# Working on the first 512 rows of expert 0 in plain fp32 between the last routing steps of a fused adaLN, scan and MoE kernel

## The reference

```python
h = _layernorm(x) * (1 + ca) + sa
x = x + ga * attn(h)          # gates, a scan over the sequence, a projection
h = _layernorm(x) * (1 + cb) + sb
x = x + gb * ffn(h)
# ffn:
gate_scores = softmax(h @ Wg + bg)
topk_scores, topk_idx = top_k(gate_scores, 2)         # renormalised
for e in range(8):
    y = gelu(h @ W1[e] + b1[e]) @ W2[e] + b2[e]       # 256 -> 1024 -> 256
    output = output + y * combine_w[..., e:e + 1]
```

## Time and profile before

| | |
|---|---|
| median of 3 runs | 806.8 us (803.32 to 809.53) |
| the profiled execution | 802.3 us, its span 800.5 us |
| PE matmul busy | 713.6 us, 89% of the span |
| DVE, ACT, POOL busy | 568.1, 408.6, 406.2 us |
| chain that ended last | PE 57%, DVE 22%, issue 10%, DMA 5%, POOL 3% |

### The profile page before, as it was taken

How to read it: one execution, slowest core, us unless ns; L and a number is a source line. 1 busy time by engine, 2 the same in 40 slices (tenths; PEclk the granted TensorE clock), 3 DMA queues, 4 the chain that set the end, 5 groups by cost and what they waited for, 6 DMA issues and landing times.

```text
span 800.5 us, 17260 instructions
## 1 busy us (share of the span) xinstructions
PE 713.6 (89%) x4850; PEld 657.7 (82%) x4850; DVE 568.1 (71%) x1793; ACT 408.6 (51%) x1024; POOL 406.2 (51%) x312
## 2 busy tenths in 40 slices
PE   4899999889799993489999899998898998989992
PEld 1777888778688873389999899998898998989992
DVE  6879899899988777665555755566875566585551
ACT  5364545435353332255655555664564664565660
POOL 1364637674744735654544544554653553554543
PEclk9899999999999997589999999999998999999997
DMA  8531104020101117334356334574542553534432
GB/s 291 179 114 54 54 5 143 14 94 28 54 22 61 47 35 237 118 100 69 69 116 131 54 62 78 114 179 106 158 64 54 118 128 56 115 57 75 66 68 41
DMA packets 50165, 72.56 MB, mean 91 GB/s; under 512 B 5792, under 2 KB 41964, under 8 KB 49968
## 3 DMA queue, kind: packets, MB, share of 16 engines
q0 software_dynamic: 16480, 27.28, 19.0%
q1 hardware_dynamic: 33616, 44.46, 17.8%
HBM read 48.85 MB, written 22.87 MB: 90 GB/s over the span
## 4 chain that ended last, share of the span: by engine, by line
PE 57%; DVE 22%; issue 10%; DMA 5%; POOL 3%; ACT 2%; SPq 0%; DVEq 0%; POOLq 0%; ACTq 0%
PE yb L913 19%; PE mm L903 19%; PE mm L759 11%; PE yb L784 3%; DMA gbr<-mod_rows,xm 3%; DVE ob L1008 2%; PE tp L886 1%; DVE rsn L941 1%; DVE bst L945 1%; DVE rt L1042 1%; DVE mm L1005 1%; DVE mm L1002 1%; DVE SL L235 1%; DVE nt L940 1%; POOL gbr L536 1%
## 5 line engine op out<-in xcount | busy, mean ns | idle before, releaser
L736 ACT ACTIVATE h<-mm,b1T 128x256 f32<-128x256 f32 (+1 forms) x288 | 134.2, 466 | 166.7 <-PE mm L903 123.4
L541 POOL DMA_INDIRECT out_x<-ysb,tokb x68 | 115.1, 1692 | 203.2 <-DVE ysb L1271 166.9
L1240 DVE TENSOR_TENSOR hl<-h,hh 128x256 fp32r<-128x256 f32 (+1 forms) x288 | 122.0, 427 | 105.0 <-ACT hh L737 102.3
L903 PE MATMUL mm<-fh,SH 128*128 128x256 f32 x576 | 165.6, 287 | 9.3 <-DVE fl L1206 9.1
L913 PE MATMUL yb<-SH,hh 128*128 128x256 f32 x544 | 158.7, 292 | 12.8 <-DVE hl L1240 12.6
L903 PE MATMUL mm<-fl,SH 128*128 128x256 f32 x576 | 163.9, 285 | 0.0
L903 PE MATMUL mm<-fh,SL 128*128 128x256 f32 x576 | 163.7, 284 | 0.0
L913 PE MATMUL yb<-SL,hh 128*128 128x256 f32 x544 | 155.1, 285 | 0.0
L913 PE MATMUL yb<-SH,hl 128*128 128x256 f32 x544 | 155.0, 285 | 0.0
L737 ACT ACTIVATE hh<-mm,b1T 128x256 fp32r<-128x256 f32 (+1 forms) x288 | 133.5, 464 | 0.0
L903 PEld LDWEIGHTS mm<-fh,SH 128*128 128x128 f32 x576 | 112.2, 195 | 11.1 <-issue 11.1
(11 more groups left out here) (206 smaller groups left out, 1203.5 us busy)
## 6 DMA issues: line engine op xcount, KB each, us to landing
xin<-disp_x SPq DMA_DIRECT2D x74, 132.0 KB
wraw<-in_L_ffn_W SPq DMA_DIRECT2D x8, 1024.0 KB, 5.3
h2all<-in_L_ffn_W SPq DMA_DIRECT2D x8, 1024.0 KB, 5.6
xb<-in_L_attn_x SPq DMA_DIRECT2D x8, 512.0 KB, 3.7
out_x<-x2b SPq DMA_DIRECT2D x8, 512.0 KB, 3.0
mb<-mod_rows SPq DMA_DIRECT2D x3, 768.0 KB, 6.2
wraw<-in_L_attn_W_ugg SPq DMA_DIRECT2D x1, 1536.0 KB, 10.2
gbr<-mod_rows,xm POOLq DMA_INDIRECT x74, 3.8
```

The costliest lines, as they stand in the source:

```text
L541: e.indirect_dma_start(out=out_rows, out_offset=bass.IndirectOffsetOnAxis(ap=tokb[:, j:j + 1], axis=0), in_=ysb[:, j, :], in_offset=None, ...
L736: e.activation(h32[:, f % 2, c_], mm[f % 4][:, c_], ACT.Gelu_apprx_tanh, bias=bias)
L903: i = e.matmul(mm[f % 4][:, 0:TE], a[:, k, f * 128:(f + 1) * 128], b[:, k, :], start=(k == 0 and t == 0), stop=(k == 1 and t == 2))
L1240: e.tensor_tensor(hl[:, f, w_], h32[:, f % 2, w_], hh[:, f, w_].bitcast(F32), ALU.subtract)\
```

## The change

Once the groups 0 to 4 have been sent, the first 512 rows of expert 0's region in `Xd` are loaded to `xinE`, and all of their work is done in plain fp32 from the raw weights (`w1raw`, `w2raw`), on PE between the routing steps of the groups 6 and 7. In stage two expert 0 starts at row `skip` = min(512, rows that it has by group 4).

- SP: `xinE` is loaded in four DMAs ahead of the last `store_x2`. The first tile of expert 0 now waits for all sends.
- PE in group 7: a count (`early_count`), and eight transposes (`turn_early`) between the two parts of `main_part(7, 3, ...)`. After `logits(6)`: seven blocks of layer 1 (`early_layer1`, 2 matmuls of 128x512), `turn_h2(7)`, the eighth block, `rank(6)`, `logits(7)`, two blocks of layer 2 (`early_layer2`, 4 matmuls of 128x256), `rank(7)`, one block, the total count, five blocks.
- ACT: two copies (`early_rows`); eight GELUs of 128x512 (`early_gelu`), each followed by one `split_high` of expert 0; `h2t_copy(7)` stands ahead of the last, and both `gate_sigmoid` behind it. 
- DVE: three small operations in `place(5)`, `early_weights` (six) ahead of `add_y(7)`, `early_out` (two of 128x512, four of 128x256) after `counts`.
- POOL: four gathers (`gbrE`) behind `send(5, 1)`, ahead of its three `split_low`; and four accumulating indirect DMAs with the early rows' results, each of which waits until the one before has landed, between `pads_done` and tile 0 of the loop.

The diff, cut to what the prediction speaks of (tile declarations, PSUM addresses and iota columns are left out):

```diff
@@ sp_program
+            e.wait_ge(S["early_known"], 1)
+            e.reg_load(r_early, skipi[0:1, 1:2])
+            e.wait_ge(S["sent0"], 16 * 8 * 4)
+            e.wait_ge(S["sent1"], 16 * 8 * (EARLY_GROUPS - 4))
...
+            for j in range(4):
+                e.reg_mov(r_block, 128 * j)
+                e.reg_alu(r_block, r_block, r_early, ALU.min)
+                e.dma_start(xinE[:, j, :], Xd[bass.ds(e.snap(r_block, min_val=0, max_val=CAP - 128), 128), :])\
+                    .then_inc(S["early_loaded"], 16)
             store_x2(NG - 1)
...
-            with e.If_ne(r_late, 0):
-                e.wait_ge(S["sent2"], 16 * 8 * 2)
-                e.wait_ge(S["counts_ready"], 1)
-                e.reg_load(r_last, nmint[0:1, 0:1])
+            e.wait_ge(S["sent1"], 16 * 8 * (EARLY_GROUPS - 4))
+            e.wait_ge(S["sent2"], 16 * 8 * (NG - EARLY_GROUPS))
+            e.wait_ge(S["counts_ready"], 1)
@@ pool_program
             send(g - 2, 1)
+            e.wait_ge(S["early_meta"], 1)
+            for j in range(4):
+                e.indirect_dma_start(out=gbrE[:, j, :], out_offset=None, in_=modd.rearrange("b (n d) -> (b n) d", d=D),
+                                     in_offset=bass.IndirectOffsetOnAxis(ap=xmE[:, j, 5:6].bitcast(I32), axis=0))\
+                    .then_inc(S["early_gb"], 16)
             for q in range(5, 8):
                 split_low(e, 0, q)
@@
             e.sem_inc(S["pads_done"], 1)
+            for j in range(4):
+                e.wait_ge(S["early_ready"], j + 1)
+                past(e, "early_sent", 16 * j)
+                e.indirect_dma_start(out=out_rows, out_offset=bass.IndirectOffsetOnAxis(ap=tokE[:, j:j + 1], axis=0),
+                                     in_=ysbE[:, j, :], in_offset=None, compute_op=ALU.add).then_inc(S["early_sent"], 16)
+            e.wait_ge(S["early_sent"], 64)
             for n in range(E):
@@ act_program
+            def early_gelu(f):
+                e.wait_ge(S["early_hidden"], f + 1)
+                if f >= 5:
+                    e.wait_ge(S["x2_ready"], NG)
+                e.activation(hE[:, f, :], mm[f % 2][:, :], ACT.Gelu_apprx_tanh, bias=vT[:, f:f + 1])\
+                    .then_inc(S["early_gelu"], 1)
@@
             h2t_copy(g - 1)
-            for q in range(8):
-                split_high(e, 0, q)
+            for f in range(NF):
+                if f == NF - 1:
+                    h2t_copy(g)
+                early_gelu(f)
+                split_high(e, 0, f)
             gate_sigmoid(g - 1)
-            h2t_copy(g)
             gate_sigmoid(g)
@@ pe_program
+            def turn_early():
+                e.wait_ge(S["early_loaded"], 64)
...
+            def early_layer1(f):
...
+                past(e, "early_gelu", f - 1)
+                for k in range(2):
+                    i = e.matmul(mm[f % 2][:, :], w1raw[:, k, f * 128:(f + 1) * 128], fE[:, k, :],
+                                 start=(k == 0), stop=(k == 1))
+                i.then_inc(S["early_hidden"], 1)
+
+            def early_layer2(f):
+                e.wait_ge(S["x2_ready"], NG)
+                e.wait_ge(S["early_gelu"], f + 1)
+                for j in range(4):
+                    i = e.matmul(yb[j // 2][:, (j % 2) * D:(j % 2 + 1) * D], hE[:, f, j * 128:(j + 1) * 128],
+                                 w2raw[:, f, :], start=(f == 0 and j % 2 == 0), stop=(f == NF - 1),
+                                 skip_group_check=True)
+                i.then_inc(S["early_summed"], 1)
@@
                 if not last:
                     turn_xn(g + 1)
+                else:
+                    turn_early()
                 main_part(g, 3, 1)
@@
             logits(g - 1)
+            for f in range(NF - 1):
+                early_layer1(f)
             turn_h2(g)
+            early_layer1(NF - 1)
             rank(g - 1)
             logits(g)
+            early_layer2(0)
+            early_layer2(1)
             rank(g)
+            early_layer2(2)
...
+            for f in range(3, NF):
+                early_layer2(f)
@@ dve_program, place
-                if g == NG - 2:
-                    e.tensor_scalar(lateint[0:1, 0:1], rt[0:1, 2, 0, 0:1], float(TE), None, ALU.is_lt)\
-                        .then_inc(S["late_ready"], 1)
+                if g == EARLY_GROUPS:
+                    e.wait_ge(S["early_counted"], 1)
+                    yield from lk(e, e.tensor_scalar(skip[:, :], tp[1][:, 0:1], float(EARLY), None, ALU.min), "dve_b")
+                    yield from lk(e, e.tensor_copy(skipi[:, 0:1], skip[:, :]), "dve_b")
+                    e.tensor_scalar(skipi[:, 1:2], tp[1][:, 0:1], -128.0, 0.0, ALU.add, ALU.max)\
+                        .then_inc(S["early_known"], 1)
@@
+            early_weights()
             add_y(g)
@@
             counts()
+            early_out()
```

More of the change, by code:

```diff
@@ L20 @@
 TE = 256
+EARLY = 512
+EARLY_GROUPS = 5
 MW = 8
@@ L140, in build @@
                 SL[i] = sb(p2, f"SL{i}", [128, 4096], F32R)
+            xinE = sb(p2, "xinE", [128, 4, DW])
+            gbrE = sb(p2, "gbrE", [128, 4, D])
+            fE = sb(p2, "fE", [128, 2, EARLY])
+            hE = sb(p2, "hE", [128, NF, EARLY])
             xin = sb(p2, "xin", [128, 2, DW])
@@ L387, in tile @@
                     load(rows_of)
-                    if first and n == 0:
-                        e.wait_ge(S["counts_ready"], 2)
-                        e.reg_load(r_last, nmint[0:1, n:n + 1])
                     if first and n + 2 < E:
                         split_done(e, n)
+                        if n == 0:
+                            e.wait_ge(S["early_summed"], NF)
                         load_w1(n + 2)
@@ L860, in pe_program @@
                     rank(g - 2)
+                if last:
+                    early_count()
                 main(g, 2)
@@ L1131, in counts, with early_weights, early_out @@
                 e.tensor_copy(kpk[:, :], kf[:, 0:2]).then_inc(S["counts_ready"], 1)
-                link(e, e.tensor_reduce(kf[:, 2:3], nf[:, 1, :], AX, ALU.min), "dve_a")
-                e.tensor_scalar(few[:, :], kf[:, 2:3], 0.0, None, ALU.is_lt).then_inc(S["few_ready"], 1)
+            def early_weights():
+                a, b, c_ = (wslE[:, q, :, :] for q in range(3))
+                e.wait_ge(S["early_loaded"], 64)
+                e.tensor_copy(xmE[:, :, :], xinE[:, :, D:DW]).then_inc(S["early_meta"], 1)
+                e.wait_ge(S["early_meta"], 1)
+                at = xmE[:, :, 2:4]
+                link(e, e.tensor_copy(tokE[:, :], xmE[:, :, 4].bitcast(I32)), "dve_a")
+                link(e, e.tensor_tensor(a, at, nomE.unsqueeze(2).to_broadcast([128, 4, 2]), ALU.is_ge), "dve_a")
+                link(e, e.scalar_tensor_tensor(b, at, float(CAP), a, ALU.is_lt, ALU.mult), "dve_a")
+                link(e, e.tensor_tensor(c_, b, xmE[:, :, 0:2], ALU.mult), "dve_a")
+                link(e, e.tensor_reduce(wE[:, :], c_, AX, ALU.add), "dve_a")
+            def early_out():
+                e.wait_ge(S["early_summed"], NF)
+                e.wait_ge(S["b2_loaded"], 16)
+                for q in range(2):
+                    e.tensor_tensor(ysbE[:, 2 * q:2 * q + 2, :], yb[q][:, :].rearrange("p (j d) -> p j d", j=2),
+                                    bc(b2b[:, 0, :], 2), ALU.add).then_inc(S["early_taken"], 1)
+                e.wait_ge(S["early_taken"], 2)
+                e.wait_ge(S["early_gb"], 64)
+                for j in range(4):
+                    e.scalar_tensor_tensor(ysbE[:, j, :], ysbE[:, j, :], wE[:, j:j + 1], gbrE[:, j, :],
+                                           ALU.mult, ALU.mult).then_inc(S["early_ready"], 1)
             weave(ln1_stats(0))
@@ L1234, in tile @@
                     if first:
-                        mark(e.tensor_scalar(nom[:, :], nom0, float(n * CAP), None, ALU.add))
+                        mark(e.tensor_scalar(nom[:, :], nom0, float(n * CAP) if n else skip[:, :], None, ALU.add))
                         due("dve_c", 1)
```

82 lines of the change are left out of this document (61 added, 21 removed).

## The result

The changed kernel takes 819.6 us (median of 4 runs, 817.95 to 820.34) where the kernel before takes 806.9 (4 runs, 803.32 to 809.53): the ratio is 1.015, 95% interval 1.011 to 1.019. The forecast was 816.5. Two executions on the third chip of the experiments, 2456.6 us of the kernel before and 905.5 us of the kernel without adds, lie far outside all others and are left out of every ratio.

A forecast was written before the change was run, and what follows sets the result against it. PE, busy 713.6 of 800.5 us with one hole at 300 to 350, where a chain of waits sets the end. -8.5 (start and tiles) + 18.2 (stall and clock) = +9.7: profiled 802.3 becomes 812, median 806.8 becomes 816.5; range 804 to 823.

The forecast's parts named there:

- three signs of being wrong or of another rival: First matmul of tile 0 after 360; group 6's first send after 329.6; clock of 0.50 within layer 1's seven blocks.
- the late sends: Rival: group 6's sends come later than booked and shift everything; +16 us, 823 us; chance 0.09.
- The stall: POOL's four chained adds delay tile 1's gathers: DVE waits 18.4 us, PE 15.9; 18.2 in the sum with the clock.
- The rival without a stall: DVE's wait is met earlier or PE's work in hand covers it; -8.5 us, 798.3 us; chance 0.12.
- that of the short stall: Adds land faster or overlap in issue, 2.7 us each; stall shrinks by 6.4, +3.3, 810 us; chance 0.14.
- Entry: PE in group 7: waiting for and turning the early rows ends the projections 1.1 us later (bounds +0.3 and +3).
- DVE's 4.29 us: A tiny DVE operation before `h2_ready_last` took 4.29 us during POOL's three `split_low`; moving these wins 4.1 us on DVE.
- ACT, the weights of group 6: `gate_sigmoid(6)` stands behind GELU 7 and a table load, so group 6's first send is at 327.6, +3.0 (bounds +1, +5).
- the table load: On ACT, the sigmoid's table must come back after the GELU; one load is 1.28 us.
- Start and tiles: Stage two: tile 0 starts at 356.8, tiles cost 11.72 us, two full tiles go; half tile starts 8.5 us earlier.
- The sum: Whole kernel: -8.5 (start and tiles) + 18.2 (stall and clock) = +9.7 us; 816.5 us on the median.

The follow-up runs named there:

- number 5: Changed kernel with both cures of the stall: the four adds right behind the last group's gather and without waits between them; 794.7 us, ratio 0.992, second chip.
- number 8: Changed kernel with two fp32 blocks ahead of group 7's turns, routing before most others, adds behind the gather and unchained; 789.2 us (second chip), 799.5 (third).
- experiment 4: Changed kernel with expert 1's two 1 MB weight loads held back until PE has signalled the eighth early hidden block; 819.9 us, ratio 1.016.

## Why the prediction came out, point by point

- **The whole, right in its range and its mechanism, with some luck in the number.** The prediction gave three signs of being wrong or of another rival, and they came: the first matmul of tile 0 after 360 (365.42), the first send of group 6 after 329.6 (336.72), and a clock of 0.50 within layer 1's seven blocks (0.50 from 318 to 322). So the late sends, which had a chance of 0.09 and 823 us, came in beside the stall. From profile to profile the miss is 8.1 us (812 forecast, 820.1 measured). The medians hide part of it, since the kernel before has a median 4.5 us above its profiled execution: 816.5 forecast, 819.6 measured.
- **The stall, right.** Forecast: DVE waits 18.4 us, PE 15.9, with the clock 18.2 in the sum. Measured: 17.8 and 16.3 in the trace, and 16.8, 19.2 and 16.9 us by leaving out or curing the adds. PE stood from 395.3 to 411.6 (forecast 386 to 402), later by the late sends. The four adds took 18.4 us until the splits start (forecast 17.2). The rival without a stall and that of the short stall are out. The estimate by the figure of the Trainium skill (DMA: Bandwidth & Descriptors, Anatomy of one DMA, SWDGE path), 2.3 us an add, is too short here too: the adds landed 3.7 to 4.7 us after issue.
- **Entry, too dear.** I booked +1.1 us. SP's four loads went out at 291.46 and the turns at 295.9 had no wait; PE's idle time before the turning of group 6 shrank from 1.22 to 0.27, and the projections began at 300.95 instead of 301.20: nothing.
- **DVE's 4.29 us, right**: with `split_low` away it was gone, and its modulation of the last group began at 313.32 instead of 317.34.
- **ACT, the weights of group 6: the order right, the size wrong in the profile after.** +3.0 us was forecast; it was +12.1 (336.72 against 324.62). The step had the order, the table load (1.28 at 332.40) and the pace right: where signals are prompt, the send is 2.2 us later than before, counted from the projections. What was missing is the first GELU's lateness, 8.5 us counted from there (15.65 against 7.16 in number 5). It makes PE stand for 7.64 us, and at the low clock the next five blocks take 2.5 us more than at number 5's pace of 1.72: 10.1 of the 10.2 us by which the send is later than in number 5.
- **Start and tiles.** I booked -8.5, from a start of tile 0 at 356.8. It was 365.42, 8.6 later, which by the prediction's own rule (each us shifts everything) leaves nothing of the gain; the profile without adds, whose tile 0 is as late, has a span of 799.8 against 800.5 before. By the medians, without the adds' cost the kernel was 4.0 us faster than before on the two chips with late signals (802.8 against 806.7 and 806.9) and, with both cures, 7.2 us faster on the one without (794.7 against 801.8).
- **The sum.** Where signals are prompt it would be 794.7 + 16.9 = 811.6 against 801.8, or +9.8; +9.7 was forecast. That is an estimate, since the changed kernel had no run there, and the close fit is again in part luck: the stall is 16.9 instead of 18.2 and the gain 7.2 instead of 8.5. Where they are late, it is +12.7 and +15.2. The kernel before is slower on those chips too, 806.8 against 801.8, by 5.0 us; number 8 is slower by 10.3 (799.5 against 789.2), and no adds there against both cures here is 802.8 against 794.7, by 8.1, if the cured adds cost nothing. So the new programs lose 3 to 5 us more on those chips than the old one, and the forecast of 816.5 fell short by 3.1. The kernel before's own profile, at 802.3 us and without a "remote" wait, looks like one with prompt signals, and the profile after doesn't: that is probably why the spans differ by 17.6 us and the medians by 12.7. It is argued, not shown, and so is that the chips differ in nothing else.

## What to carry to other kernels

A chain of DMAs on the queue engine costs its landings, not its issues: here four adds held GpSimd for 18.4 us chained and 9.6 unchained. Put unchained where the engine was idle anyway, they left VectorE no wait over 1.7 us for its gathers. Ask for each wait on such an engine what is queued behind it: here a gather, for which VectorE waited, for which TensorE waited, and that took more than the 4 to 7 us that the change had gained. Work put in a hole must not stand ahead of the step that ends the hole: with the routing first and only two blocks ahead of it, and the adds cured, the same idea gives 0.984 of the kernel before on the second chip (0.992 with the cures alone) and 0.991 on the third.

## What the hardware showed unexpectedly

In the nine profiles of the first and the third chip and of the first result, TensorE's signal after fp32 work came long after its records: the first GELU started at 316.5 to 318.7 us. In the four profiles of the second chip no wait ends with "remote", and the GELU started at 309.2 to 310.3 in the three that have it there. In seven of the nine a second place is `early_out`, whose wait also ends with "remote" (13.3 us, off the path); in the two with the routing first it is ACT's wait for the later blocks (12.15 and 12.91 us).

The traces hold more on this than the places above. They record when a semaphore was updated, besides when an instruction ran. I counted the updates of TensorE and VectorE that come over 0.25 us after the end of the instruction that makes them, up to 780 us. In the nine profiles these are 32 to 42 of TensorE's some 450 updates, 7.6 to 8.9 us late at most, spread over the whole program, stage two too, and 1 to 3 of VectorE's, up to 1.2 us late. In the profile before and in the four of the second chip there is none, and the largest lag is 0.04 us. So it is neither fp32 work alone nor TensorE alone. In eight of the nine, one of VectorE's waits for its own operation ends within 0.1 us of the start of an early GELU, as in the two rows of the profile after. The nine also hold fewer updates, some 7000 against 9133 to 9206, though all instruction records are there; what that means isn't known.

It isn't the two weight loads (experiment 4), or not mainly. Whether TensorE really finished later or only said so later stays open: in the changed kernel the granted clock fell to 0.50 by 312, before the signal, while in experiment 4 it was still 1.00 at 316. Also open is whether the same costs the kernel before its 5 us: it has no profile with late signals. Each chip was used in one session, so chip and session can't be told apart. A time taken on one chip is to be compared only with one from the same chip: 789.2 and 799.5 us are the same kernel.
